# Reordering the first sequences of a fused attention and feed-forward kernel: squares behind the same tile's transposes, earlier second rows of x, later first queries, and the last layer-norm statistics ahead of the outputs

## The reference

```python
x = x + xattn(layernorm(x), ctx_1024, mask, ...)   # 4 heads of 128 against one key and one value head
x = x + attn(layernorm(x), ...)                    # 16 causal heads of 32 over 64 rows
x = x + ffn(layernorm(x), ...)                     # 512 -> 2048, gelu, layer norm, 2048 -> 512

def xattn(x, mem_seq, mem_mask, rms_scale, q_w, kv_w, out_w):
    xn = rmsnorm(x, rms_scale)
    mn = rmsnorm(mem_seq, rms_scale)               # 1601 context rows per sequence, 512 wide
    q = einsum('BTD,NDH->BTNH', xn, q_w)
    k, v = einsum('BSD,cKDH->cBSKH', mn, kv_w)
    q = rope(q, positions) * 128 ** -0.5
    k = rope(k, positions)
    probs = softmax(where(mem_mask, q @ k, -2.38e38))
    return einsum('BTNH,NHD->BTD', probs @ v, out_w)
```

## Time and profile before

| what | value |
|---|---|
| median of 3 runs | 1067.03 us (1064.93 to 1068.35) |
| the profiled execution: its own time, its span | 1066.37 us, 1064.4 us |
| busy: PE, DVE, ACT, POOL | 930.7, 668.4, 505.0, 375.6 us |
| granted TensorE clock, mean | 0.97 of full speed |
| PE idle at the head | 1.3 us at 22.3, 5.9 us at 30.1 |
| last matmul of the kernel ends | 1054.3 us |
| last DVE instruction ends | 1057.6 us |

### The profile page before, as it was taken

One profiled execution on the slowest core, in us unless ns is written; L12 is line 12 of the kernel. 1 busy time (PEld: TensorE's weight loads), 2 busy tenths in 40 slices (PEclk: granted clock), 3 DMA queues, 4 the chain that ended last, 5 costly groups with the idle time before them and its releaser, 6 DMA issues. The chain is left out here.

```text
span 1064.4 us, 22549 instructions
## 1 busy us (share of the span) xinstructions
PE 930.7 (87%) x7307; PEld 700.7 (66%) x7307; DVE 668.4 (63%) x1334; ACT 505.0 (47%) x1059; POOL 375.6 (35%) x506
## 2 busy tenths in 40 slices
PE   3798879898888888878979999999889999999996
PEld 2787667686676776657968887888765444444443
DVE  5577756766766777676366566766656538475543
ACT  4565445654455554544333333433446455555542
POOL 3354444444444444440022111211103325444434
PEclk9899989999999999988989999999989999999998
DMA  6621223211222322331355543444422102012011
GB/s 178 184 76 56 80 88 86 87 54 57 76 86 73 97 74 76 115 115 41 90 160 140 149 126 108 127 124 108 118 60 76 55 1 88 32 40 70 21 60 43
DMA packets 100318, 93.02 MB, mean 87 GB/s; under 512 B 45424, under 2 KB 61904, under 8 KB 100176
## 3 DMA queue, kind: packets, MB, share of 16 engines
q1 hardware_dynamic: 99376, 90.96, 29.2%
q10 hardware_dynamic: 672, 0.26, 0.1%
q0 software_dynamic: 128, 0.03, 0.0%
HBM read 74.37 MB, written 12.66 MB: 82 GB/s over the span
## 5 line engine op out<-in xcount | busy, mean ns | idle before, releaser
L255 PE MATMUL bank<-f,f 128*128 128x256 f32 (+4 forms) x5032 | 637.8, 300 | 68.8 <-issue 26.0
L255 PEld LDWEIGHTS bank<-f,f 128*128 128x128 f32 (+3 forms) x5032 | 460.9, 160 | 196.5 <-issue 80.8
L244 DVE TENSOR_TENSOR f<-bank,f 128x512 fp32r<-128x512 f32 x211 | 140.5, 683 | 47.7 <-ACT f L241 45.8
L241 ACT ACTIVATE f<-bank 128x512 fp32r<-128x512 f32 x211 | 121.1, 591 | 88.8 <-PE bank L230 83.6
L230 PE MATMUL bank<-f,f 128*128 128x128 f32 x896 | 132.5, 279 | 33.7 <-DVE f L244 13.0
L230 PEld LDWEIGHTS bank<-f,f 128*128 128x128 f32 x896 | 102.9, 143 | 56.1 <-issue 31.3
L1248 PE MATMUL bank<-f,f 128*128 128x512 f16 x512 | 123.1, 384 | 0.0
L1221 POOL TENSOR_TENSOR f<-f,f 128x512 f32<-128x512 f32 x59 | 75.1, 1273 | 132.9 <-ACT f L1216 132.9
L1226 DVE SCALAR_TENSOR_TENSOR f<-bank,f,f 128x512 f16<-128x512 f32 x64 | 48.0, 750 | 92.0 <-ACT f L1208 75.8
L463 POOL TENSOR_TENSOR f<-f,f 128x512 f32<-128x512 f32 x32 | 42.0, 1311 | 160.9 <-ACTq L75 138.9
L954 POOL TENSOR_TENSOR f<-f,f 128x512 f32<-128x512 f32 x32 | 33.4, 1043 | 177.4 <-DVE f L951 177.4
(11 more groups left out here) (138 smaller groups left out, 995.6 us busy)
## 6 DMA issues: line engine op xcount, KB each, us to landing
f<-in_ctx_dram SPq DMA_DIRECT2D x71, 256.0 KB, 2.8
f<-x_scratch SPq DMA_DIRECT2D x64, 256.0 KB, 3.8
x_scratch<-f SPq DMA_DIRECT2D x32, 256.0 KB, 2.0
f<-in_L_ffn_W_fc_dram SPq DMA_DIRECT2D x32, 256.0 KB, 2.9
f<-in_L_ffn_W_proj_dram SPq DMA_DIRECT2D x32, 256.0 KB, 3.4
f<-in_x_dram SPq DMA_DIRECT2D x31, 256.0 KB, 2.9
f<-in_ktab_dram SPq DMA_DIRECT2D x71, 64.0 KB, 2.0
f<-f SPq DMA_DIRECT2D x64, 64.0 KB, 2.4
```

The lines of the kernel that those rows point to most:

```text
L241: return maybe("act", lambda e: e.activation(hi, src, ACT.Copy), sem(name + "_hi"), waits, when)
L244: return maybe("dve", lambda e: e.tensor_tensor(lo, src, hi.bitcast(F32), ALU.subtract), sem(name + "_lo"), waits, when)
L255: f = lambda e, i=i, a=a, b=b: e.matmul(dst, a, b, start=(first and i == 0), stop=(last and i == n - 1), skip_group_check=check)
```

## The change

Four things are moved, and nothing is computed otherwise:

- For sequences 0, 1 and 2, the square of tile j goes from slot s0 - 5 + j (order 0.3) to slot s0 - 2 + j (order 1.5), behind the transposes and the high part of the same tile. The buffer of the tile is given back only after both.
- `load_xq(1)` goes from slot -4, behind the loads of sequences 0 to 2, to slot -11 between the loads of sequences 0 and 1. The masks of sequences 0 and 1 are loaded in slot -11 too, behind sequence 1 (they were in slots -1 and 8), and the bias of sequence 0 is made in slot 4 and not in slot -1.
- The product of the first queries, `stage_Q2(0)`, goes from slot -3 to slot 1, and `stage_Q3(0)` from slot -1 to slot 3, both at order 8. The four `scaled_lo` instructions for the query weights go from the preparation to slots -1 and 0, two in each, at order 4.
- At the end, `s3_stat` sums the squares before the sums and waits for each alone, and the first two row tiles of the last but one step of the second product (four matmuls) go from ahead of `s3_stat` to behind it, so that the sixteen matmuls left run row tile by row tile.

```diff
@@ stage_square(b, t)
         if t == FT - 1:
             done["ssq", b] = done["sq"]
+            if b <= 2:
+                cx_free[b].append(done["sq"])
@@ stage_T(b, j)
         if j == FT - 1:
-            cx_free[b] = [tt, done["ssq", b]]
+            cx_free[b] = [tt, *([done["ssq", b]] if b > 2 else [])]
@@
+    def first_masks():
+        for b in range(2):
+            done["msk", b] = load_mask(b)
+
     def stage_mask(b):
         u = b % 2
-        t = load_mask(b)
+        t = done["msk", b] if b < 2 else load_mask(b)
@@
-    def scaled_lo(src, hi, lo, waits, ths):
-        for c in range(4):
+    def scaled_lo(src, hi, lo, waits, ths, chunks=range(4)):
+        for c in chunks:
@@
     stage_Q1b(0)
-    tw1["q"] = scaled_lo(wq_t, WQh, WQl, [t_wq, t_r1], t_qh)
     side[0] = Q
     ahead = [(s, s.n) for s in sems.values()]
+
+    def stage_WQ(c):
+        tw1["q"] = scaled_lo(wq_t, WQh, WQl, [t_wq, t_r1], t_qh, [c])
+
     for c in range(4):
+        at(-1 + c // 2, 4, lambda c=c: stage_WQ(c))
         at(5 + c, 9, lambda c=c: stage_Wo(c))
     at(3, 9, load_wo)
+    at(-11, 2.65, first_masks)
@@
-        at(s0 + 4 if b > 0 else -1, 1.7, lambda b=b: stage_mask(b))
+        at(s0 + 4, 1.7, lambda b=b: stage_mask(b))
         for j in range(FT):
-            at(s0 - 5 + j, 0.3, lambda b=b, j=j: stage_square(b, j))
+            at(s0 - (5 if b > 2 else 2) + j, 0.3 if b > 2 else 1.5, lambda b=b, j=j: stage_square(b, j))
@@
             if i:
-                at(s0 - 12, 1.4, lambda i=i: load_xq(i))
+                at(s0 - 12 if i > 1 else -11, 1.4 if i > 1 else 1.65, lambda i=i: load_xq(i))
                 at(s0 - 7, 1.4, lambda i=i: stage_Q0(i))
@@
-            at(s0 - 3, 8, lambda i=i: stage_Q2(i))
-            at(s0 - 1, 8, lambda i=i: stage_Q3(i))
+            at(s0 - 3 if i else 1, 8, lambda i=i: stage_Q2(i))
+            at(s0 - 1 if i else 3, 8, lambda i=i: stage_Q3(i))
@@
     def s3_plast():
-        for t in (2, 3):
-            s3_p(last - 1, [t])
         for t in range(4):
-            s3_p(last, [t])
+            for q in (last - 1, last):
+                s3_p(q, [t])
@@ s3_stat(g)
-        w = [*tok["acc", g], *tok["acc2", g], *gfree[k], t_on]
-        for t in range(4):
-            for z in range(2):
+        w = {1: [*tok["acc2", g], *gfree[k], t_on], 0: tok["acc", g]}
+        for z in (1, 0):
+            for t in range(4):
@@
-    at(H0 + last + 2, 2.1, lambda: s3_p(last - 1, [0, 1]))
```

More of the change, by code:

```diff
@@ L1281, in s3_stat @@
                         bank[k][:, z * 4 + t:z * 4 + t + 1], a, ones[:, 0:1], start=n == 0, stop=n == m,
-                        skip_group_check=True), sem("f_p") if t == 3 and z and n == len(parts) - 1 else None,
-                        w if t + z == 0 else ())
+                        skip_group_check=True), sem("f_p") if t == 3 and not z else None,
+                        w[z] if t + n == 0 else ())
         tok["stat", g] = [tk]
```

## The result

| what | before | after |
|---|---|---|
| median of 15 runs each, taken together | 1065.57 us (1063.69 to 1068.35) | 1069.45 us (1065.94 to 1073.26) |
| ratio, 95% interval | | 1.0034 (1.002 to 1.0048) |
| the profiled execution: own time, span | 1066.37, 1064.4 us | 1072.08, 1070.2 us |
| granted TensorE clock, mean | 0.97 | 0.97 |

The changed kernel is 0.34% slower, some 3.6 us. The forecast was 1069.1, with a range that holds the measured time. That it came within 0.4 us is in part luck: the medians that are compared here lie 3.9 us apart and not 2.1, and the 2.1 had been added to a median of the kernel before that was 1.5 us higher (1067.03, of three runs). And the trace shows that two falls of the clock were paid at the head where the forecast had one, which is the course which the prediction gave to its second rival.

The account below looks back on a forecast made before the run. Bound by head waits on the second x rows (PE 5.87, DVE 7.61 us) and slow clock, then by DVE and ACT from 50 to 60. Terms +0.5 + 2.0 - 0.4 = +2.1 gave median 1069.1 us, range 1063.2 to 1072.6.

Parts of the forecast that it names:

- second rival: Slow clock twice: the clock also falls after PE's idle time at 29.6; sum +4.5, 1071.5 us; chance 0.27.
- clock behind that: Head, after PE's 3.7 us idle for bank NM: a fall is hidden by the weights' wait if under 1.6 us.
- output weights landed: Slot 5: load issued at 37.2, 6.1 us to landing, so 43.3; leaves 5.2 of the 6.9 us ahead.
- from there to Q0(2): Slots 5 to 9, DVE: 10.2 us against 9.0 before, with three more squares on ACT; gain left 4.0 us.
- from there to the second logits: Slot 9, DVE: high part awaited until 7.1 us after Q0(2) starts, second logits' reduction 0.6 later, at 61.8.
- ACT's wait for r(2): Slot 9: copies of KV(2,1) wait for r(2), behind Q0(2)'s chain on POOL, some 5.9 us up to 59.
- second logits against before: Slot 9: reduction starts at 61.8 against 61.27, the 4.0 us gain gone and 0.5 lost; term +0.5.
- slow clock behind slot 9: After PE's 4.9 us idle from 59.0 to 63.9, the clock falls; term +2.0, bounds 0 and 2.4.
- end: Outputs' last three instructions start at 1055.2 against 1055.54; term -0.4, or -0.7 if the clock holds, +0.8 at worst.
- gain of the x rows: Head: waits of 7.6 and 5.9 us and up to 2.4 us of slow clock go; gross gain 8.3 us at most.
- three waits for r(b): ACT L446 waits for POOL L275 near 27, near 39 and, longest, some 5.9 us up to 59.
- rival without a wait for r(2): Slot 9: r(2) ready when ACT reaches the copies, PE not idle; sum -4.4, 1062.6 us; chance 0.17.

Follow-up runs that it names:

- e2: The kernel before with only the loads of the second x rows and the first masks moved (first bias in slot 4); ratio 0.9985, median 1063.1 us.
- e6: The kernel before with x rows and masks early, output weights' load in slot -11 and the new end, squares and first queries unmoved; ratio 0.9915, 1056.08 us.
- e10b: The same kernel as e6, run once more against the kernel before; ratio 0.9935, median 1058.89 us.
- e4: The kernel before with the new end alone, squares' statistics first and sixteen matmuls behind them; ratio 0.9994, median 1064.49 us.
- e3: The changed kernel with the output weights' load moved from slot 3 to slot -11; ratio 1.0009 against the kernel before, median 1067.41 us.
- e7: The changed kernel with r(0) and r(2) ahead of Q0's chains on POOL and the output weights' load in slot -11; ratio 0.9965 against before, 1061.68 us.
- e1: The changed kernel with r(0) and r(2) ahead of Q0's chains on POOL, nothing else altered; ratio 0.9985 against the kernel before, 1063.2 us.
- e8: e7 with stage_Q3(0) in slot 2 instead of slot 3; ratio 0.9918 against the kernel before, median 1057.12 us.
- e11: e8 with the squares of sequence 2 alone back in their old slots; ratio 0.9983 against the kernel before, median 1063.85 us.

## Why the prediction was right, point by point

| step | forecast | measured |
|---|---|---|
| Q0(1) on DVE, no wait for x | about 22 | 22.14 |
| first copies wait for r(0) until | 26.9 | 27.25 |
| PE idle for bank NM up to | 33.3 | 34.27 |
| clock behind that | hidden | 0.50, 2.97 us lost |
| end of the second queries' product | 40.2 | 44.1 |
| output weights landed | 43.3 | 45.3 |
| DVE's low part of them | 43.95 | 46.17 |
| from there to Q0(2) | 10.2 us | 10.1 us |
| Q0(2) | 54.1 | 56.28 |
| from there to the second logits | 7.7 us | 7.6 us |
| ACT's wait for r(2) | 5.9 us | 5.81 us |
| second logits against before | +0.5 | +2.6 |
| slow clock behind slot 9 | 2.0 | 2.3 |
| end | -0.4 | -0.7 |
| sum | +2.1 | +4.2 |

**What held.** The mechanism in slot 9 and at the waits of the head. The gain of the x rows was put at 8.3 at most and is 8.2 to 8.4 (e2 and e6). The three waits for r(b) are there: the first 3.48 us for 4.2, the second at 42.34 and not near 39, the third 5.81 us for 5.9 (5.7 to 5.8 by the prediction's own steps). The two walks through queues, 10.2 and 7.7 us, were right to 0.1 us, since they were added up from durations of rows on engines whose order is written out. The Trainium skill, "TensorE: Matmul & The Clock Gate", in its note on engine queue depths, has ACT and DVE take their queues strictly in order; by that rule the trace agrees, 5.81 us of ACT and 4.90 of DVE behind one late value.

**What was off.** Two terms. The first is the landing of the output weights: the load was issued at 37.16, as forecast (37.2), but took 8.2 us and not the 6.1 of the earlier trace rows.

```profile
f<-in_L_xattn_out_w_dram SPq DMA_DIRECT2D x1, 1024.0 KB, 8.2
```

The same megabyte took 6.0 to 8.4 us in the fourteen traces. The edits are not needed to explain the spread: e6 and e10b are one kernel, and in that order they say

```profile
f<-in_L_xattn_out_w_dram SPq DMA_DIRECT2D x1, 1024.0 KB, 6.0
```

```profile
f<-in_L_xattn_out_w_dram SPq DMA_DIRECT2D x1, 1024.0 KB, 7.6
```

The kernel before and e4, with the same head, took 6.1 and 7.4. The row that was read was near the lower end; one row of one trace was taken for a constant, and its bounds were not in the sum.

The second is the clock behind the first idle time. It was called hidden as long as it cost under 1.6 us. It cost 2.97, as the clock fell after 3.05 us of idle time, a pause whose shortness (3.7 us and not 5.9) the prediction had held against a fall. The two lie beside each other: ACT waits for the weights until 45.3, DVE is done with the queries' rotation at 46.17, so that the clock ended up as the later of the two. How much this fall costs varies from trace to trace, and no run shows that an edit decides it. In e3 the pause is 3.48 us and the clock is at 0.50 only from 34.7 to 38.1, with 3.40 us of PE work (1.70 lost), and in e7 it is 3.05 us and nothing is lost; the 1.3 us less of e3 is most of what its rotation is ahead.

A smaller slip is in the bound of the end: 0.216 us per matmul is not what 1044.55 to 1047.31 gives for twelve, which is 0.230. Only the +0.8 hangs on it.

**Which case it was.** Rival two said: the product ends at 42.6 to 43.6, DVE takes up the weights' low part at 45.8, slot 9 costs 2.3, the second fall 2.4 to 2.7, the end gives 0.4, sum +4.5. Measured: 44.1, 46.17, 2.6, 2.3, 0.7, sum +4.2. That is the course of events; it had been given 0.27, and the forecast's course 0.40. The time came out near the forecast because the kernel before ran 1.5 us below the median of its first three runs; that is luck, and of the change itself 2.1 us were forecast and 3.6 to 3.9 measured. The rival without a wait for r(2), chance 0.17, is refuted by the 5.81 us in after, which e1 shows to be that wait.

**What is left.** The steps above make +4.2 us, the medians 3.6 to 3.9, the two profiled executions 5.7. The profiled execution of after lies 2.6 us above the median of its runs and that of before 0.8, which is the difference between 5.7 and 3.9. Along the traces the delay is 4.9 us at Q0(3), 2.3 at Q0(6) (168.91 and 171.23), 3.9 at Q0(8) (227.39 and 231.24) and 6.2 at the last group of eight L255 (1042.82 and 1049.04). Falls of the clock at other places in each trace are a part of that (below); the way from Q0(8) on was not followed.

## What to carry to other kernels

When a step is moved to a later slot, follow its result through every queue it passes, the small ones on POOL too: a value of 128x4 that used to be three slots early held ACT for 5.8, DVE for 4.9 and PE for 4.7 us, and the clock took 2.3 more. When an early stall is taken away, list what the queues wait for next and move that in the same edit: the x rows alone gave 1.8 us, with the output weights also early 8.2. And where the profile names a releaser, look whether another result became ready at that same moment; swapping two steps on one queue told which it was. A duration that goes into a sum wants more than one trace: the same load took 6.0 and 7.6 us in two executions of one kernel.

## What the runs showed of the hardware

**The same program, another place of the slow clock.** The traces of e6 and of its repeat, e10b, are of one kernel. From 82 to 86 us, in that order:

```profile
82.00:86.00 4.00, 3.32 (x25) 2.93 (x26) 2.62 (x6) 3.48 (x10) 2.55 (x3) 1.00 0.46 135
```

```profile
82.00:86.00 4.00, 3.27 (x15) 2.91 (x16) 2.62 (x6) 3.47 (x11) 2.22 (x3) 0.58 0.57 136
```

PE is busy about as long in both, but in the second the clock falls and fewer matmuls fit in. The pauses of PE just before are the same (0.94 and 0.97 us). The way from Q0(3) to Q0(4) is 28.67 us instead of 27.20. In e8 and its repeat it fell there too, in after and in e11 it did not. A fall that one trace shows at a place need not be in the median run, and this one moves a single trace by 1.5 us. It was not expected that the clock also falls without a long idle time: in before it is at 0.50 from 139.7 to 143.1, and the longest pause of PE in the ten microseconds ahead of that is 1.16 us.

```profile
139.70:143.10 3.40, 3.40 (x10) 2.62 (x9) 1.64 (x5) 0.42 (x1) 2.48 (x9) 0.50 0.01 2
```

The same group of matmuls in before and in after, where it comes 4.9 us later:

```profile
139.04 4.59 PE L255 MATMUL bank<-f,f 128*128 128x512 f32 x12 [1.16 <-DVEq L75]
```

```profile
143.95 3.05 PE L255 MATMUL bank<-f,f 128*128 128x512 f32 x12 [1.08 <-DVEq L75]
```

In after this stretch is run at 1.00, with nearly the same pause ahead of it. Before has one more such stretch, 0.50 from 150 to 153; in after the clock there, 4.9 us later, is 1.00. Of the delay of 4.9 us, which Q0(5) still shows (138.98 and 143.89), 2.3 are left at Q0(6) (168.91 and 171.23).

**One pause, three outcomes.** At the wait for bank NM, PE is idle for 3.05 us in after, 3.04 in e1, 3.48 in e3 and 3.05 in e7. Behind it 5.93 us of work run at 0.50 in after, 6.08 at 0.51 in e1, 3.40 at 0.50 in e3 and none in e7. What decides between them is open; a fall behind a pause of this size is a chance to be given, in these traces three times out of four.

**The end at full clock.** The sixteen matmuls behind the statistics take 3.61 us in after and in e4, 0.226 each, where the twelve of before took 4.28, 0.357 each, at a granted clock of 0.62 from 1050.0 to 1054.3. The forecast had taken 0.357 for all, and the prediction's own bound for a clock that holds was the -0.7 that was measured.
